# A whole decoder step on one core: a new order in the first attention pair, in the routing, and in the final loads

## What is computed

```python
q, k, v = latents @ Wq, kv @ Wk, kv @ Wv          # kv = concat(context, latents), 32 heads on 8 kv heads
x = x + tanh(g) * (softmax(rms(q) @ rms(k).T / sqrt(128)) @ v) @ Wo
x = x + tanh(g) * trunc(clip(down(trunc(silu(gate) * up)) ))   # ternary weights, INTER = 1376
x = x + tanh(g) * softmax(context @ q3.T) @ context            # second cross attention
x = x + tanh(g) * (shared(xn) + sum of the top 2 of 16 experts(xn))   # routed mixture of experts
```

## Time and profile before

| what | us |
|---|---|
| median of 3 runs | 1215.84 |
| lowest and highest | 1215.38, 1218.82 |
| the profiled execution's own time | 1218.76 |
| its span | 1217.0 |
| TensorE busy | 1172.9 |
| VectorE busy | 821.9 |
| ScalarE busy | 580.1 |
| GpSimd busy | 327.6 |

### The profile page before, as it was taken

How to read it: one execution, slowest core, us unless ns; L and a number is a source line. 1 busy time by engine, 2 the same in 40 slices (tenths; PEclk the granted TensorE clock), 3 DMA queues, 4 the chain that set the end, 5 groups by cost and what they waited for, 6 DMA issues and landing times.

```text
span 1217.0 us, 20678 instructions
## 1 busy us (share of the span) xinstructions
PE 1172.9 (96%) x6912; PEld 1003.2 (82%) x6912; DVE 821.9 (68%) x2379; ACT 580.1 (48%) x1351; POOL 327.6 (27%) x287
## 2 busy tenths in 40 slices
PE   7999999999999999999999999999999999899994
PEld 6888888888889888888888888887787777577782
DVE  7767677666666766676676776678788878673333
ACT  5645455444545545455454555445443455433431
POOL 5403022120312312132030221203333403234531
PEclk8999999999999999999999999999999999999997
DMA  7001000000101101010110000002122213852316
GB/s 277 1 36 52 2 36 19 35 34 0 52 0 34 39 13 34 0 52 0 34 52 0 34 0 1 1 1 54 57 78 78 57 63 95 318 196 79 91 44 239
DMA packets 36266, 69.65 MB, mean 57 GB/s; under 512 B 5858, under 2 KB 22242, under 8 KB 34166
## 3 DMA queue, kind: packets, MB, share of 16 engines
q1 hardware_dynamic: 31014, 57.96, 14.0%
q0 software_dynamic: 3760, 8.40, 2.2%
q10 hardware_dynamic: 1440, 2.62, 0.6%
HBM read 60.57 MB, written 12.32 MB: 60 GB/s over the span
## 4 chain that ended last, share of the span: by engine, by line
PE 59%; DVE 20%; issue 9%; ACT 5%; DMA 3%; POOL 3%; SPq 1%; DVEq 0%; ACTq 0%; POOLq 0%
PE bank L374 14%; PE bank L376 14%; PE bank L375 14%; PE bank L2043 5%; PE bank L1904 3%; ACT probs L822 3%; DVE probs L1196 3%; PE bank L1747 2%; PE bank L2055 2%; DVE iq L1361 2%; DVE k_junk L1151 2%; DVE row_max L1169 2%; DVE pt_lo L1183 2%; POOL k_rstd L613 1%; PE bank L1689 1%
## 5 line engine op out<-in xcount | busy, mean ns | idle before, releaser
L822 ACT ACTIVATE probs<-bank,exp_bias,q_rstd 128x256 f32<-128x256 f32 x256 | 141.0, 561 | 136.4 <-DVE exp_bias L1177 136.4
L1188 DVE TENSOR_TENSOR o_lo<-bank,o_hi 128x512 fp32r<-128x512 f32 x64 | 44.3, 692 | 180.0 <-ACT o_hi L815 180.0
L374 PE MATMUL bank<-wkv_hi,kv_src_lo 128*128 128x256 f32 x512 | 146.2, 286 | 1.6 <-DVE kv_src_lo L1221 1.6
L376 PE MATMUL bank<-wkv_hi,kv_src_hi 128*128 128x256 f32 x512 | 146.0, 285 | 0.0
L375 PE MATMUL bank<-wkv_lo,kv_src_hi 128*128 128x256 f32 x512 | 145.8, 285 | 0.0
L617 POOL TENSOR_TENSOR q_rstd<-q_var,minus_half 128x8 f32<-128x8 f32 x32 | 52.4, 1637 | 301.9 <-DVE q_var L1156 301.9
L811 ACT ACTIVATE pt_hi<-bank 128x512 fp32r<-128x512 f32 x128 | 69.6, 596 | 116.4 <-PE bank L1747 116.4
L374 PE MATMUL bank<-wo_hi,o_lo 128*128 128x512 f32 x256 | 105.0, 410 | 1.6 <-DVE o_lo L1188 1.2
L374 PE MATMUL bank<-wq_hi,kv_src_lo 128*128 128x512 f32 x256 | 102.9, 402 | 1.3 <-issue 1.3
L376 PE MATMUL bank<-wo_hi,o_hi 128*128 128x512 f32 x256 | 102.1, 399 | 0.0
L375 PE MATMUL bank<-wo_lo,o_hi 128*128 128x512 f32 x256 | 101.5, 396 | 0.0
(11 more groups left out here) (272 smaller groups left out, 3043.4 us busy)
## 6 DMA issues: line engine op xcount, KB each, us to landing
weights<-r_w SPq DMA_DIRECT2D x16, 768.0 KB, 9.3
wq_raw<-wq SPq DMA_DIRECT2D x8, 1024.0 KB, 4.8
wo_raw<-wo SPq DMA_DIRECT2D x8, 1024.0 KB, 4.8
wkv_raw<-wkv SPq DMA_DIRECT2D x8, 512.0 KB, 3.3
y_back<-y_dram SPq DMA_DIRECT2D x8, 512.0 KB, 6.5
gu_raw<-w_gate SPq DMA_DIRECT2D x10, 256.0 KB, 3.4
gu_raw<-w_up SPq DMA_DIRECT2D x10, 256.0 KB, 3.9
wd_raw<-w_down SPq DMA_DIRECT2D x10, 256.0 KB, 4.2
```

The lines of the kernel that those rows point to most:

```text
L374: eng.matmul(out_ap, a_lo, b_hi, start=start, stop=False)
L376: return eng.matmul(out_ap, a_hi, b_hi, start=False, stop=stop)
L822: act.activation(probs[:, h, :], scores_ps[h // 2][:, (h % 2) * 256:(h % 2) * 256 + 256], ACT.Exp, bias=exp_bias[:, h:h + 1], scale=q_rstd ...
L1188: dve.tensor_tensor(o_lo[:, par, :], o_ps[:, :], o_hi[:, par, :].bitcast(F32), ALU.subtract)\
```

## The change

Four parts, cut to what moves:

1. Start. TensorE gets 5 dummy transposes between the first two rows and 14 behind them, both key halves stand ahead of `turn_pair(1)`, `turn_pair(2)` goes behind the first query transposes, and `turn_pair(3)` into group 0, tile 1. VectorE takes the first group's `wkv_low` and one of four `wq_low`; the last two x tiles' statistics and rows go behind the first `bias_of`. GpSimd's `ln_root(6)` and `(7)` stand behind all context subtractions, and its first context subtraction waits for row 5.
2. `moe_rows` has three buffers; the shared chunks are placed further ahead, one of expert 1 before the last row's turn.
3. Token table first: `gather_tokens` has 16 columns and waits for it alone, the selection and offsets follow, the places come in `gather_places` behind `outer(4)`. VectorE takes `hidden_low(3)` from GpSimd; `add_shared(4)` and `(5)` stand before `take_weights`. The first four gathered rows have a place of their own. Expert 1 is loaded when the rows are turned and stored.
4. Final loads: six loads, alternately from SP and ScalarE, none waiting for another.

```diff
+LOADS = ((0, 1), (1, 1), (2, 2), (4, 2), (6, 1), (7, 1))
...
+        def load_y(eng, some):
+            for i in range(2):
+                eng.wait_ge(y_stored[i], 16 * ((TILES + 1 - i) // 2))
+            for n in some:
+                t, count = LOADS[n]
+                eng.dma_start(y_back[:, t:t + count, :],
+                              y_dram[t * TOP * P:(t + count) * TOP * P, :].rearrange("(t p c) n -> p t (c n)", t=count, c=TOP))\
+                   .then_inc(y_loaded[n], 16)
...
@@ sync
             load_weights(2, 4)
+            sp.wait_ge(ln_transposed[1], NB)
+            rows_are_stored(sp)
+            load_weights(1, 2)
             sp.wait_ge(h_done, 4 * SHARED)
             load_weights(4, 7)
-            sp.wait_ge(tokens_done, 1)
-            load_weights(1, 2)
...
+            load_y(sp, range(0, len(LOADS), 2))
@@ gpsimd
             ln_root(0)
             ln_root(1)
-            wkv_low(0)
+            wq_low(0, range(0, 2))
             ln_root(2)
             ln_root(3)
-            wq_low(0)
+            wq_low(0, range(2, 3))
             ln_root(4)
+            k_root(0)
             ln_root(5)
-            k_root(0)
+            pool.wait_ge(ln_row_ready[0], 6)
             ctx_low(1)
-            ln_root(6)
-            ln_root(7)
             q_root(0, 0)
             ctx_low(2)
             ctx_low(3)
+            ln_root(6)
+            ln_root(7)
...
             hidden_low(2)
-            hidden_low(3)
             pool.wait_ge(tokens_ready, 1)
@@ scalar
+            kv_high(0, 0, 0)
             ctx_high(1)
-            kv_high(0, 0, 0)
+            kv_high(0, 1, 0)
             key_source_high(2)
             key_source_high(3)
-            kv_high(0, 1, 0)
...
+            load_y(act, range(1, len(LOADS), 2))
@@ vector
             rows_pair(0)
+            first_wkv_low()
...
             low_pair(0)
             stats_pair(1)
+            first_wq_low(R - 1)
+            v_low(0, 0, 0)
             rows_pair(1)
-            stats_pair(2)
-            v_low(0, 0, 0)
+            dve.wait_ge(x_loaded[2], 16)
+            ln_stats_of(4, 4)
+            k_norm(0)
+            v_low(0, 1, 0)
             low_pair(1)
-            v_low(0, 1, 0)
-            k_norm(0)
-            rows_pair(2)
...
-            stats_pair(3)
             q_norm(0, range(0, 1))
-            rows_pair(3)
+            ln_stats_of(5, 5)
+            rows_pair(2)
             k_low(0, 0)
             q_low(0, 0, 0)
+            q_low(0, 1, 0)
             q_norm(0, range(1, 2))
-            q_low(0, 1, 0)
-            low_pair(2)
...
                     bias_of(n, b)
                     if isinstance(g, int) and g == 0 and b == 0:
+                        low_pair(2)
+                        stats_pair(3)
+                        rows_pair(3)
+                    if isinstance(g, int) and g == 0 and b == 1:
                         low_pair(3)
...
             hidden(2)
+            start_slots()
+            places()
             step_ranges()
-            places()
+            take_tokens()
             hidden(3)
-            take_tokens()
+            take_selection()
+            take_offsets()
+            hidden_low(3)
+            step_places()
             take_biases()
+            take_places()
+            add_shared(4)
+            add_shared(5)
             take_weights(0)
             take_weights(1)
-            add_shared(4)
-            add_shared(5)
@@ tensor
-            turn_pair(0)
+            turn_rows(0)
+            keep_clock(5)
+            turn_rows(1)
+            keep_clock(14)
             kv_half(0, 0, 0)
+            kv_half(0, 0, 1)
             turn_pair(1)
-            kv_half(0, 0, 1)
             q_half(0, 0, 0)
             q_tile(0, 1, first_q)
-            turn_pair(2)
             turn_k(0)
             turn_q(0, range(0, 1))
+            turn_pair(2)
             pe.wait_ge(k_lo_ready, 1)
             turn_q(0, range(1, 2))
-            turn_pair(3)
...
                     scores(g, b, 1)
+                    if isinstance(g, int) and g == 0 and b == 1:
+                        turn_pair(3)
...
+                    if isinstance(g, int) and g == 0 and b == 1:
+                        pe.wait_ge(ln_lo_ready[0], NB)
                     if after_start(g, b, 1):
                         weigh_values(g, b - 1)
...
                 if s == NB + 1:
                     pe.wait_ge(ln_hi_ready[0], 3 * NB)
-                    inner_part(0, 1, range(0, 2))
+                    inner_part(0, 1)
+                    pe.wait_ge(ln_lo_ready[1], NB - 1)
+                    inner_part(1, 0, range(0, 1))
...
-            inner_part(0, 1, range(2, KC))
-            pe.wait_ge(ln_lo_ready[1], NB - 1)
-            inner_part(1, 0, range(0, 1))
+            inner_part(1, 0, range(1, 2))
             turn_logits(0)
-            inner_part(1, 0, range(1, 2))
+            inner_part(1, 0, range(2, 3))
             route(1)
-            inner_part(1, 0, range(2, 3))
+            inner_part(1, 0, range(3, KC))
+            inner_part(1, 1, range(0, 1))
             turn_logits(1)
-            inner_part(1, 0, range(3, KC))
-            pe.wait_ge(ln_lo_ready[1], NB)
-            inner_part(1, 1)
+            inner_part(1, 1, range(1, KC))
...
-            turn_selection()
             turn_gates()
             outer(0)
             outer(1)
             outer(2)
             gather_tokens()
+            turn_selection()
             outer(3)
-            for t in range(4, NB):
+            gather_offsets()
+            outer(4)
+            gather_places()
+            for t in range(5, NB):
                 outer(t)
```

More of the change, by code:

```diff
@@ L186, in build @@
         q3 = put("q3", [P, KC, P])
-        sim = put("sim", [P, P])
         rows_at = at[0]
@@ L208, in build @@
         x_cols = put("x_cols", [P, BLOCKS * D])
+        at[0] = start + 12 * D * 4
+        first_x_rows = put("first_x_rows", [P, 4, D])
         at[0] = start + 8 * D * 4
@@ L243, in build @@
         at[0] = here
+        sim = put("sim", [P, P])
+        at[0] = here
         r_pick = put("r_pick", [P, TOP, NB, E])
@@ L314, in build @@
         diagonal_ready, summed, sum_copied = sem("diagonal_ready"), sem("summed"), sem("sum_copied")
-        rows_stored = [sem(f"rows_stored{i}") for i in range(2)]
+        rows_stored = [sem(f"rows_stored{i}") for i in range(3)]
         maps_ready = sem("maps_ready")
-        chosen_ready, ranks_done, sel_step = (sem(n) for n in ("chosen_ready", "ranks_done", "sel_step"))
+        rank_step, sel_step = (sem(n) for n in ("rank_step", "sel_step"))
         offset_ready = sem("offset_ready")
@@ L326, in build @@
         y_stored = [sem(f"y_stored{i}") for i in range(2)]
-        y_loaded = [sem(f"y_loaded{i}") for i in range(PAIRS)]
+        y_loaded = [sem(f"y_loaded{i}") for i in range(len(LOADS))]
         r_added = sem("r_added")
@@ L370, in build, with rows_of, rows_are_stored, load_of @@
         dve_tiles = [t for t in range(NB) if t not in PE_TILES]
+        def rows_of(j):
+            return (first_x_rows if j < 4 else x_rows)[:, j % 4, :]
+        def rows_are_stored(eng):
+            for i in range(3):
+                eng.wait_ge(rows_stored[i], 16 * len(range(i, NB, 3)))
+        def load_y(eng, some):
[6 more added lines that the diff above has]
+                   .then_inc(y_loaded[n], 16)
+        def load_of(t):
+            return max(n for n, (first, _) in enumerate(LOADS) if first <= t)
         def three(eng, out_ap, a_hi, a_lo, b_hi, b_lo, start, stop):
@@ L596, in wkv_low, with wq_low @@
                                        ALU.subtract).then_inc(wkv_lo_ready, 1)
-            def wq_low(g):
-                for h in range(R):
+            def wq_low(g, heads=range(R)):
+                for h in heads:
                     cols = slice(h * HD, h * HD + HD)
@@ L854, in _ @@
             k_high(0, 0)
[L855 removed]
+            q_high(0, 0)
             key_source_high(4)
             key_source_high(5)
[L858 to L860 removed]
+            ctx_high(2)
             ctx_high(3)
@@ L1040, in _ @@
                 act.activation(gate_t[:, half * D:half * D + D], bank[half][:, :], ACT.Copy).then_inc(gate_step, 1)
-            for i in range(2):
-                act.wait_ge(rows_stored[i], 8 * NB)
+            rows_are_stored(act)
             shared_rows(0)
@@ L1565, in hidden, with hidden_low @@
                                          in1=e_h[:, n % 2, :], op0=ALU.add, op1=ALU.mult).then_inc(h_ready, 1)
+            def hidden_low(n):
+                e, half = shared_order[n]
+                dve.wait_ge(h_hi_ready, n + 1)
+                dve.tensor_tensor(h_lo[:, e, half, :], e_h[:, n % 2, :], h_hi[:, e, half, :].bitcast(F32),
+                                  ALU.subtract).then_inc(h_lo_ready, 1)
             def add_shared(t):
@@ L2022, in gather_tokens, with gather_places @@
                           stop=True).then_inc(tokens_done, 1)
+            def gather_places():
```

(6 more changed lines are left out.)

146 lines of the change are left out of this document (76 added, 70 removed).

## The result

| | before | after |
|---|---|---|
| median of 20 runs each, us | 1217.51 | 1219.91 |
| lowest and highest | 1214.80, 1220.29 | 1217.84, 1222.60 |
| the profiled execution's own time | 1218.76 | 1222.48 |
| its span | 1217.0 | 1220.7 |

The ratio of after to before is 1.0018, with a 95% interval of 1.0011 to 1.0026: 2.4 us slower by the medians. The kernel before came out at 1217.51 over 20 runs, not at the 1215.84 of three from which I forecast. Moved by that difference, the top of my range would be 1218.2 instead of 1216.5, and 1219.91 still lies above it; the sign is wrong whatever the base.

What follows compares the result with a forecast made beforehand. TensorE, busy 96% of the span, bounds the kernel; only its waits or lower-clock stretches can shrink. First pair 1.0, routing -2.9 and final loads -0.7 sum to -2.6 from 1215.84: 1213.2 us, range 1208.8 to 1216.5.

Steps and rivals of the forecast that it cites:

- register loads 1.1: Last step of the routing chain: after outer(7) ends at 1096.0, register loads take 1.1 us, routed loop starts at 1097.1.
- Up to outer(7) the sum: Routing chain: outer(4) at 1087.8, places to 1091.1, outer(5), (6), (7) at 1.65 us each, ending at 1096.0.
- first pair: Start, 0 to 54 us: 4 us won early become a TensorE wait and half clock; +1.0 us, bounds -4 to +2.
- zero if anything pins the loop's start: Upper bound for row buffers and token table together, whose range was -4.5 to 0 us.
- -2.9: Routing: row buffers and token table together start the routed loop at 1097.1 instead of 1100.04 us.
- Final loads: Tail: six loads issued by about 1198, the end at about 1216.3; -0.7 us, bounds -2.3 to +1.
- (a): Rival, start: the first pair keeps its gain, -2.4 us in place of +1.0, total 1209.8; 24%.
- (b): Rival, start: only the clock holds, the first pair gives +0.1 us, total 1212.3; 13%.
- (c): Rival, routing: VectorE's longer queue pins the routed loop's start, 1.5 of the 2.9 us stay, total 1214.6; 11%.
- (d): Rival, start: TensorE stays at half clock until saturated at 54, +9.4 us, in all +5.8, total 1221.6; 4%.
- The rule of the Trainium skill: Start: by it the 19 dummy transposes hold no clock, turned probabilities come 3 us later than forecast, total 1216.2; 3%.

Runs made afterwards that it cites:

- e4: Changed kernel with four register reads instead of eight, put behind the first two turned rows of the routed loop; 1214.56 us, ratio 0.9983 to the kernel before.
- e10: Changed kernel with the same eight register reads spread, two ahead of each of outer(5), (6), (7), two behind the turned rows; 1216.01 us, 0.9985 of the kernel before.
- e11: Changed kernel with sixteen register reads instead of eight ahead of the routed loop; one run, first routed matmul 10.33 us behind outer(7)'s end against 4.75.
- e6: Changed kernel with VectorE making the last pair's rows behind k_norm, GpSimd's order kept; one run, turned probabilities at 37.95 and 52.19 us against 40.09 and 55.16.
- e7: Changed kernel with the final loads as before: eight, all from SyncE, the last four each behind a landing; 1221.06 us, ratio 1.0025 to the kernel before.
- e3: Changed kernel with 38 dummy transposes in TensorE's idle time ahead of the first turned probabilities; 1218.93 us, ratio 1.0015 to the kernel before.
- e2: Changed kernel with GpSimd waiting for exp_bias before its last context subtractions and VectorE making the last rows behind k_norm; 1217.89 us, 1.0003 of the kernel before.
- e8: Changed kernel with GpSimd's wait for exp_bias, the last rows behind k_norm, and four register reads put late; 1212.88 us, ratio 0.9954 to the kernel before.
- e14: Changed kernel with the last rows behind k_norm and four register reads put late, without GpSimd's wait; 1213.35 us, ratio 0.9960 to the kernel before.

## Why the prediction was wrong

**The failed step is "register loads 1.1".** I had taken the 1.10 us of issue ahead of the loop for the price of the reads, and added it to outer(7)'s end. It was the rest of 5.4 us, of which 4.4 were hidden behind ten slow matmuls. When the change made outer(7) faster, as forecast, the cover shrank to 2.35 us and the same reads showed 3.43 us. The loop's start was not outer(7)'s end plus a constant but the end of a chain of reads that begins when the last matmul is handed over. e4, e10 and e11 show it. Up to outer(7) the sum was right: it had 1096.0 for its end without the first pair's share, and the profile has 1098.35 less 2.39, again 1096.0. From +2.39 at the second turned probabilities the difference goes to -0.58 there, -3.0; then the reads put +2.3 on it.

**The bound was wrong too.** I let this part range from -4.5 to 0, "zero if anything pins the loop's start". But a longer idle time also cost the clock: 0.50 in 1104 to 1106, 1.63 us over the first 32 products, and 0.3 later on. The forecast knew this mechanism, and used it for the first pair only. So -2.9 became +1.3 (from +2.39 at the second turned probabilities to +3.71 at the loop's end: -3.0, +2.3 and +2.0). That the last 2.0 are the clock's is read from the windows, and from e4, where the clock stays at 1.00 and the same 32 products take 3.84; no run filled this gap alone.

**First pair: the mechanism right, the size not.** Clock 1.00 from the start, key halves done near 16.1, exp_bias held over 2 us, a gap of 4.46 us for 4.4, half clock behind it: all as written. Each link was some tenths late: turned probabilities at 40.09 for 39.5, key transposes at 45.69 for 44.5, scores at 56.30 for 55.2. The part cost +2.1 for +1.0; the bound of +2 was just missed. e6 shows what I had in the chain but did not see as the decision: VectorE makes the last rows, for which nobody hurries, ahead of the normalisation for which TensorE waits.

**Final loads:** -0.7 forecast, 0.0 in the profiled pair (24.5 us from the loop's end both times), and e7 finds nothing to tell. The chain that ends last in after runs through TensorE's two tiles, as forecast, and is longer than forecast (after, critical chain):

```profile
1210.09 3.78 PE bank L2231 x4
1213.87 1.71 PE bank L2228 x2
1215.58 2.02 PE bank L2231 x4
1217.62 0.60 ACT x_sb L1100
```

It took 7.5 us for the 6.3 in the sum, and began 13.9 us behind the loop's end, for 13.2.

**The rivals.** (a) and (b) are out, the pair lost time. (c), the pinned start, was right in kind and had 11%, but named VectorE's queue; it was TensorE's own sequencer. (d), the one slower case, put the loss at a half clock lasting until 54; the windows have less than 1.00 from 38 to 46 only. No case had two moderate losses together, which is what came. The rule of the Trainium skill, TensorE: Matmul & The Clock Gate, Part 4: PE-mode transpose, that the full clock does not engage for transposes, doesn't hold here: the window of 9 to 10 us, all dummy transposes, has 1.00, and e3's 38 kept 1.00 through a gap that otherwise ended at 0.50.

## What to carry to other kernels

An idle time of "issue" in a trace is what is left of a chain after its cover; before you speed up what lies ahead of it, look for the sequencer's own records and ask when the chain starts, not when it ends. Reads of registers for dynamic addresses go where matmuls have just been handed over, two at a time, never eight in a row ahead of an urgent matmul. And a gain at the start of a pipeline is easily lost in the next queue: here 4 us at 17 us had become a loss at 40, until VectorE's queue was put in the order in which the results are needed.

## What the runs showed of the hardware

- A register read of TensorE from SBUF costs its sequencer 0.64 to 0.67 us (e11, sixteen in a row), though its record is 0.30 long. Some ten matmuls of 128x512 had been handed over ahead in both kernels, and they alone hide it: 4.4 us at half clock, 2.35 at full.
- The length of the idle time alone doesn't say whether the clock falls. In e2 it fell behind 2.09 us, in e6 it stayed behind 3.00 (e8 and e14 repeat this with 2.08 and 3.01; TensorE was busy without a break in the 4 us ahead of the idle time each time), windows of e2 and then of e6 (PE busy and the rest, then the clock; in e6 PE alone):

```profile
38.00:40.00 2.00, 2.00 (x15) 2.00 (x14) 1.97 (x13) 1.09 (x2) 0.54 (x1) 0.69 0.00 0
40.00:42.00 2.00, 2.00 (x11) 2.00 (x11) 1.54 (x6) 0.00 (x0) 0.73 (x1) 0.50 0.00 0
```
```profile
38.00:40.00 2.00, 2.00 (x18) 1.00 0.04 8
40.00:42.00 2.00, 1.49 (x14) 1.00 0.00 0
```

- A VectorE instruction of 128x4 with both operands in SBUF took 2.36 us beside GpSimd's subtraction in after, 0.16 in e2, where GpSimd waited for it. The normalisation of 128x256 from SBUF was held too, 1.63 us instead of 0.34 for its first instruction in e2. Not every instruction is: ln_stats beside the same subtraction took 0.69 us as elsewhere (e2, 33.03 and 34.04).
